# Nucleus search of attention rows: partial sums at two guessed points per row in place of three constants

## The reference

```python
def _adj_from_feats(Xa, W1, W2, W3):
    logits = (Xa @ W1) @ W2 @ (Xa @ W3).T
    idx = jnp.argsort(-logits, axis=1)
    csum = jnp.cumsum(jax.nn.softmax(jnp.take_along_axis(logits, idx, axis=1), axis=1), axis=1)
    k_i = jnp.sum(csum < 0.9, axis=1) + 1            # entries kept in this row
    keep = the k_i largest of each row
    return jax.nn.softmax(jnp.where(keep, logits, -jnp.inf), axis=1)
for s in range(2):
    A = _adj_from_feats(Xa, W1, W2, W3)
    Xf = Rf @ Xf;  Xb = Rb @ Xb;  Xa = A @ Xa
    Z = Z + (Xf @ U1[s] + Xb @ U2[s] + Xa @ U3[s])
```

## Time and profile before

| | |
|---|---|
| time, median of 3 runs | 3638.87 us (3638.29 to 3641.05) |
| span of the profiled execution | 3639.0 us |
| TensorE busy | 3175.4 us (87%) |
| VectorE busy | 2635.1 us (72%) |
| ScalarE busy | 1889.6 us (52%) |
| GpSimd busy | 996.2 us (27%) |
| L1345, evaluations, VectorE | 778.0 us, x208 |
| L1022, sums, ScalarE | 958.7 us, x312 |
| L1368 and L1378, extraction, VectorE | 586.9 us, x81 each |

### The profile page before, as it was taken

The page is one execution under the profiler, slowest core; times in us unless marked ns, Lnnn a source line. Parts: engine busy times, 40 slices in busy tenths (PEclk is TensorE's granted clock), DMA queues, the critical chain, the costliest instruction groups (busy, mean ns, idle before and its releaser), DMA issues. The chain is left out here.

```text
span 3639.0 us, 40362 instructions
## 1 busy us (share of the span) xinstructions
PE 3175.4 (87%) x13212; PEld 2289.6 (63%) x13212; DVE 2635.1 (72%) x3794; ACT 1889.6 (52%) x2355; POOL 996.2 (27%) x2293
## 2 busy tenths in 40 slices
PE   4999899987999999999875878667899889996799
PEld 3788688875677776777633445344555555554688
DVE  6963400006999999999839999999999999998100
ACT  2211311218788787888744556545565556563100
POOL 1212411211122221212211334334434334334211
PEclk9999999988999999999987989888999999998899
DMA  6544444432122221212221111111122222222255
GB/s 251 209 156 137 129 154 162 160 119 64 51 67 61 55 69 56 67 56 56 58 82 39 51 48 44 45 40 49 51 80 63 68 78 58 76 81 75 69 196 179
DMA packets 142416, 328.49 MB, mean 90 GB/s; under 512 B 15457, under 2 KB 95393, under 8 KB 130977
## 3 DMA queue, kind: packets, MB, share of 16 engines
q1 hardware_dynamic: 142240, 326.31, 28.3%
HBM read 287.59 MB, written 38.67 MB: 90 GB/s over the span
## 5 line engine op out<-in xcount | busy, mean ns | idle before, releaser
L1345 DVE SCALAR_TENSOR_TENSOR U<-E,trial 128x3327 f32<-128x3327 f32 x208 | 778.0, 3740 | 0.0
L880 PE MATMUL bank<-Hc,PT 128*128 128x256 f32 x2704 | 647.0, 392 | 68.8 <-ACT PT L1062 68.8
L880 PEld LDWEIGHTS bank<-Hc,PT 128*128 128x128 f32 x2704 | 528.0, 197 | 194.4 <-ACT PT L1062 92.3
L920 PE MATMUL bank<-big,adj 128*128 128x512 f32 x1352 | 613.7, 605 | 0.0
L1022 ACT ACTIVATE junk<-E,neg_3c 128x3327 uint8<-128x3327 f32 x156 | 479.1, 3071 | 5.1
L1022 ACT ACTIVATE junk<-E,neg_c 128x3327 uint8<-128x3327 f32 x156 | 479.6, 3074 | 1.7
L920 PEld LDWEIGHTS bank<-big,adj 128*128 128x128 f32 x1352 | 254.9, 194 | 329.4 <-issue 327.6
L893 PE MATMUL tr<-ident,E 128*128 128x128 f32 x1352 | 200.3, 291 | 275.5 <-DVE E L1394 275.5
L1062 ACT ACTIVATE PT<-tr 128x1024 f32<-128x1024 f32 x208 | 176.9, 851 | 369.2 <-PE tr L893 369.2
L893 PEld LDWEIGHTS tr<-ident,E 128*128 128x128 f32 x1352 | 172.8, 151 | 305.9 <-DVE E L1394 287.4
L920 PE MATMUL bank<-Hc,adj 128*128 128x256 f32 x1352 | 319.1, 388 | 0.0
(11 more groups left out here) (231 smaller groups left out, 4481.7 us busy)
## 6 DMA issues: line engine op xcount, KB each, us to landing
adj<-adjT SPq DMA_DIRECT2D x131, 448.0 KB, 3.4
E<-adjT SPq DMA_DIRECT2D x32, 1664.0 KB, 7.0
adj<-adjT SPq DMA_DIRECT2D x104, 384.0 KB, 3.4
adj<-adjT SPq DMA_DIRECT2D x20, 1664.0 KB, 7.0
adj<-adjT SPq DMA_DIRECT2D x14, 1216.0 KB, 5.7
E<-adjT SPq DMA_DIRECT2D x13, 1216.0 KB, 5.8
xt<-xin SPq DMA_DIRECT2D x52, 128.0 KB, 5.8
x_d<-xn SPq DMA_DIRECT2D x52, 128.0 KB, 1.7
```

The costliest lines, as they stand in the source:

```text
L880: last = mm(axp[:, 0:D], PT[k % 2][:, h, i * P:(i + 1) * P], Hc[:, j], start=(k == 0 and h == 0 and i == 0), stop=(k == SLOTS - 1 and h == ...
L920: last = mm(agg[:, 0:w], adj[:, j], rhs[:, j], start=(j == 0), stop=False)
L1345: V_.scalar_tensor_tensor(out=U[:, 0:N], in0=e, scalar=point, in1=e, op0=ALU.is_ge, op1=ALU.mult, accum_out=found))
```

## The change

ScalarE's six sums over E become four: Relu and Sign at two points, which are different for each row. GpSimd makes the first point (`guess`) from the mean of the scores, the maximum and the sum of exponentials, as soon as the exponential is done; after the first two sums it corrects it (`update(t, 0)`), ScalarE sums at the second point in slot 2, and `update(t, 1)` gives bracket and first point to VectorE. The mean comes from accumulators on the four copies of the scores. Slot 0 has no sums any more. VectorE evaluates 3 and 4 times, not 3 and 5, aims a little higher in step 1, and takes the mass above the upper end from an accumulator of L1355. GpSimd's order in a round changes: the 128x256 sums of z, y, x2 first, then `guess`, then the LayerNorm steps, `update(F, 0)`, the rest of the y LayerNorm, the z sums of step 0, `update(F, 1)`, and last the two 128x256 instructions of the output.

```diff
-EVALS = (3, 5)
-AIM = 3.0
-KEEP_END = 0.8
-FIXED = (0.008, 0.03, 0.1)
+EVALS = (3, 4)
+SUMS = 4
+POINTS = 2
+SHIFT = (1.4, 0.0)
+STEER = (2.0, 4.0)
+AIM = (3.0, 4.0)
+KEEP_END = (0.8, 0.75)
...
@@ ScalarE
-                        def fixed(t, lo, hi):
...
+                        def sums(t, j):
+                            act.wait_ge(aimed, POINTS * t + j + 1)
+                            for m, (func, acc_) in enumerate(((ACT.Relu, over), (ACT.Sign, sign))):
+                                before = SUMS * t + 2 * j + m
+                                if before >= 1:
+                                    act.wait_ge(summed, before)
+                                go(junk[:, 0:N], E[:, t % 3, 0:N], func, bias=negp[:, t % 2, j:j + 1], scale=1.0,
+                                   accum_out=acc_[:, t % 2, j:j + 1]).then_inc(summed, 1)
...
-                                    go(halves(E[:, L % 3])[:, :, c0:c0 + w], lg[:, :, 0:w], ACT.Copy).then_inc(lg_copied, 1)
+                                    go(halves(E[:, L % 3])[:, :, c0:c0 + w], lg[:, :, 0:w], ACT.Copy,
+                                       accum_out=musum[:, L % 2, k:k + 1]).then_inc(lg_copied, 1)
...
-                                    fixed(F, 0, 2)
...
-                                        fixed(F, 2, 4)
+                                        sums(F, 0)
...
-                                        fixed(F, 4, 2 * NF)
+                                        sums(F, 1)
...
@@ GpSimd
+                        def offer(t, j):
+                            then(ts(negp[:, t % 2, j:j + 1], p, -UNDER, None, ALU.mult))
+                            pool.sem_inc(aimed, 1)
...
+                        def prepare(step):
+                            then(ts(up_(0), p, STEER[step], ga_(12), ALU.mult, ALU.add),
+                                 ts(up_(1), p, AIM[step], ga_(12), ALU.mult, ALU.add),
+                                 ts(up_(2), p, RIDGE[step], None, ALU.mult))
+                            then(tt(up_(3), up_(2), up_(2), ALU.mult))
+                            then(tt(up_(4), up_(3), ga_(11), ALU.mult))
...
+                        def guess(t):
...
+                            pool.wait_ge(exp_done, t + 1)
...
+                            then(tt(ga[:, 0:2], musum[:, q, 0:2], musum[:, q, 2:4], ALU.add),
+                                 tt(ga_(2), z, root, ALU.pow))
+                            then(tt(ga_(3), ga_(0), ga_(1), ALU.add),
+                                 ts(ga_(4), ga_(2), ROOT, -ROOT - math.log(N), ALU.mult, ALU.add))
+                            then(ts(ga_(5), ga_(3), 1.0 / N, nm, ALU.mult, ALU.add))
+                            then(tt(ga_(6), ga_(4), ga_(5), ALU.subtract))
+                            then(ts(ga_(7), ga_(6), 2.0, 0.01, ALU.mult, ALU.add),
+                                 ts(ga_(8), ga_(5), 1.0, -SHIFT[step], ALU.mult, ALU.add))
+                            then(tt(ga_(9), ga_(7), half, ALU.pow),
+                                 tt(ga_(10), ga_(8), ga_(7), ALU.add))
+                            then(ts(ga_(13), ga_(9), -QUANTILE, ga_(10), ALU.mult, ALU.add))
+                            then(ts(ga_(14), ga_(13), -0.001, -36.0, ALU.min, ALU.max))
+                            then(tt(p, e_, ga_(14), ALU.pow))
+                            offer(t, 0)
...
+                        def update(t, j):
...
+                            pool.wait_ge(summed, SUMS * t + 2 * (j + 1))
+                            then(ts(count, sign[:, q, j:j + 1], 0.5, N / 2, ALU.mult, ALU.add))
+                            then(ts(mass_, count, p, over[:, q, j:j + 1], ALU.mult, ALU.add))
+                            then(tt(up_(15), mass_, up_(0), ALU.add),
+                                 tt(gap_p, mass_, up_(1), ALU.add),
+                                 ts(took[:, 1:2], mass_, tgt, None, ALU.is_ge))
+                            if j > 0:
...
+                                then(tt(ga_(11), up_(18), up_(19), ALU.mult))
...
+                            then(tt(up_(22), e_, up_(20), ALU.pow),
+                                 tt(ends, parts[:, 0], parts[:, 1], ALU.add))
+                            then(tt(up_(23), up_(22), p, ALU.mult))
+                            if j < POINTS - 1:
+                                then(ts(p, up_(23), hi, lo, ALU.min, ALU.max))
+                                offer(t, j + 1)
+                                prepare(step)
+                            else:
+                                then(ts(point, up_(23), hi, lo, ALU.min, ALU.max))
+                                pool.sem_inc(bracketed, 1)
...
+                            if F is not None:
+                                guess(F)
+                            if Y is not None:
+                                pool.wait_ge(ln3_a, 2 * Y + 1)
+                                tt(st3(1), st3(0), ln_const[:, 0:1], ALU.mult).then_inc(ln3_p, 1)
+                                ln_tail(st3, ln3_p, ln3_a, Y)
+                            if second(X):
+                                pool.wait_ge(ln_a, 2 * b + 1)
...
+                            if F is not None:
+                                update(F, 0)
+                            if second(X):
+                                ln_tail(st, ln_p, ln_a, b)
...
+                            if F is not None:
+                                update(F, 1)
...
@@ VectorE
-                            then(V_.tensor_copy(mass[:, 0:1], hi[:, 2:3]),
-                                 V_.memset(E[:, t % 3, N:NP], 0.0),
+                            then(V_.memset(E[:, t % 3, N:NP], 0.0),
                                  V_.scalar_tensor_tensor(out=U[:, 0:N], in0=e, scalar=hi[:, 0:1], in1=e,
-                                                         op0=ALU.is_ge, op1=ALU.subtract, reverse1=True))
+                                                         op0=ALU.is_lt, op1=ALU.mult, accum_out=sc[:, 5:6]))
+                            then(V_.tensor_tensor(mass[:, 0:1], Zs[:, q:q + 1], sc[:, 5:6], ALU.subtract))
```

More of the change, by code:

```diff
@@ L17 @@
+import math
 from contextlib import ExitStack, contextmanager
@@ L78, in pipeline @@
         static(u)
-def between_floats(value):
-    t = np.float32(3 * value)
-    while True:
-        t = np.nextafter(t, np.float32(np.inf))
-        near = [np.float32(t / np.float32(3))]
-        for _ in range(2):
-            near = [np.nextafter(near[0], np.float32(0))] + near + [np.nextafter(near[-1], np.float32(np.inf))]
-        if all(np.float32(3) * e != t and 3 * float(e) != float(t) for e in near):
-            return float(min(e for e in near if 3 * float(e) > float(t))), float(t)
 def build(nc, n_nodes, xin, adjT, W0T, b0, W1g, A1T, A2, A3, UA, UB, UC, gamma, beta, tin, Wg3, out):
@@ L1168, in _ @@
[L1168 to L1188 removed]
+                        ts = G_.tensor_scalar
@@ new lines, in _, with then @@
+                        pool.wait_ge(step_done, len(values))
+                        pool.sem_clear(step_done)
+                        root, minus, half, e_ = (known[:, i:i + 1] for i in range(4))
+                        ga_ = lambda a: ga[:, a:a + 1]
+                        up_ = lambda a: up[:, a:a + 1]
+                        p, gap_p = cand[:, 0:1], cand[:, 1:2]
+                        n = [0]
+                        def then(*ins):
+                            for i in ins:
+                                i.then_inc(step_done, 1)
+                            n[0] += len(ins)
+                            pool.wait_ge(step_done, n[0])
@@ L1189, in bracket @@
+                        def guess(t):
+                            q, step = t % 2, t // NT
+                            restart()
+                            z, nm = Zs[:, q:q + 1], nmax[:, q:q + 1]
+                            tgt, below = (trial2[:, q, a:a + 1] for a in (GOAL, BELOW))
+                            pool.wait_ge(exp_done, t + 1)
                             if t >= 2:
                                 pool.wait_ge(probs_ready, t - 1)
[L1192 to L1196 removed]
@@ L1197, in bracket @@
-                            then(tt(mid[:, :, 2], ft[:, 0], ft[:, 1], ALU.add))
-                            then(tt(mid[:, :, 1], mid[:, :, 2], tgt.to_broadcast([P, NF]), ALU.subtract),
-                                 tt(below, tgt, share[:, 4:5], ALU.mult),
-                                 G_.tensor_scalar(met[:, 1:NF + 1], mid[:, :, 2], tgt, None, ALU.is_ge))
-                            for i in range(2, NF + 1):
-                                then(tt(met[:, i:i + 1], met[:, i:i + 1], met[:, i - 1:i], ALU.mult))
@@ new lines, in guess @@
+                            then(tt(shape4(parts[:, 0]), zz, shape4(outset[:, 0]), ALU.mult),
+                                 ts(tgt, z, P_NUC, None, ALU.mult),
+                                 ts(ga_(12), z, -P_NUC, None, ALU.mult),
+                                 tt(ga_(15), z, minus, ALU.pow))
+                            then(tt(ends2[:, q], parts[:, 0], outset[:, 1], ALU.add),
```

(6 more changed lines are left out.)

200 lines of the change are left out of this document (81 added, 119 removed).

## The result

The changed kernel takes 3690.6 us (median; 3682.1 to 3691.2), the kernel before 3638.8 us beside it: a ratio of 1.0135 (95% interval 1.0120 to 1.0149), 52 us slower. The sign and the chain through GpSimd held; the loss was forecast five times too large. The profiled execution has a span of 3689.4 us, 50.5 more than the kernel before.

What follows compares the result with a forecast made beforehand. It took step 0 to be held by TensorE and VectorE, step 1 by VectorE. Adding +208 us for step 0, +41 for step 1 and 10 for first rounds to 3639 gave 3898, say 3900 us, range 3710 to 4030.

Steps and rivals of the forecast that it cites:

- The sign: Whole kernel: the change makes it slower, chance 0.86.
- the chain through GpSimd: Both steps: ScalarE's sums wait for GpSimd's guess and update, holding up TensorE and VectorE; +208 us and +41 us.
- The port rule: VectorE and GpSimd: a GpSimd instruction starting under a 3327-wide scalar_tensor_tensor ends with it; free under MAX8, MATCH_REPLACE, row maximum.
- The lengths of step 1's rounds: Step 1, search to search: 57.3 us with one extraction, 56.1 with two, 61.4 with three.
- Rival 2: GpSimd's steps cost only their own durations; chain 32.5 us, below TensorE's 36.54; 3519 us, chance 0.12.
- Rival 3: Points worse than the constants with one evaluation more: three extractions in every tile; 4160 us, half of that 4030; chance 0.06.
- Rival 1: The chain shows in step 0 only, step 1's longer search covers it; 3735 us, chance 0.10.
- the price of guess in step 0: GpSimd in step 0: guess up to its offer is 10 dependent steps, three with pow, 5.3 us.
- VectorE's windows: Step 0: guess advances only in 1.6 us gaps between evaluations, offer at 19.0 us; +208 us, 48 without windows so well filled.
- the case of cheaper steps: GpSimd's tensor_scalar at 0.19 us: some 2 us less per round over 50 rounds, -100 us.
- +41 forecast: Step 1: 1451 us against 1410 over 25 intervals; the saved evaluation is eaten by the chain.
- a second extraction would be nearly free: Step 1: a second extraction is covered by the chain; 56.1 us a round with two, 57.3 with one.

Runs made afterwards that it cites:

- act_tail_ln: Changed kernel with the first LayerNorm step ahead of guess and guess's last two steps (exponential, product) made by ScalarE; 3581.3 us, ratio 0.9831.
- cap_one: Changed kernel with exactly one extraction per tile and evaluations as tensor_scalar reading E once, counting entries, so not searching the right value; 3352.2 us.
- pad2: Changed kernel with two more dependent 128x1 multiplications in guess ahead of its last pow, 0.54 us of GpSimd work per tile; 3834.8 us, ratio 1.0540.
- cap_nowait: Changed kernel with exactly one extraction per tile and ScalarE's sums at constants 0.03 and 0.1, waiting for nothing of GpSimd, whose instructions all stay; 3544.5 us.
- best: act_tail_ln with GpSimd's three 128x256 instructions of y1 moved from ahead of guess to behind update(F, 0); 3576.6 us, ratio 0.9826.
- new_35: Changed kernel with EVALS = (3, 5), the evaluation given back in step 1; 3804.7 us, ratio 1.0450.
- ln_first: Changed kernel with one 128x1 GpSimd instruction, the first LayerNorm step of tile Y, moved ahead of guess; 3637.9 us, ratio 0.9994 to the kernel before.

## Why the prediction was wrong, and what of it held

**What held.** The port rule, read from three rows, holds in every run. In the kernel after, 229 of 230 GpSimd steps of at most six columns that started under a 3327-wide scalar_tensor_tensor, with over 0.7 us of it left, ended with it or later (the exception started 0.02 us after it; in no run did one get through that started more than 0.03 us after), and under MAX8, MATCH_REPLACE and the row maximum none took more than 0.57 us. The chain from the exponential over guess, sums, update, sums, update to the search holds, with its parts at the places named: ScalarE waits for the offer, the row maximum waits for the score copy, TensorE for PT. The lengths of step 1's rounds from search to search came out within 0.8 us, for one, two and three extractions. Rival 2 (faster, 3519 us) fell; act_tail_ln (3581 us) came nearest to it among the versions that do the whole search. Rival 3 fell: fewer extractions, not more. Rival 1 came nearest in time (3735 us), by amounts that were not the measured ones: it had +208 in step 0 and -112 in step 1, the runs +59 and -17.

**The step that failed: the price of guess in step 0, and with it the place of the offer in VectorE's windows.** I put 5.3 us on guess and 0.39 on each dependent tensor_scalar. Free of the port, guess takes 4.85 us, with tensor_scalars of 0.19 to 0.27 us and 0.08 behind each (cap_one). Half a microsecond is small, but the walk made of it an offer at 19.0 us into the search, caught under L1355, and hence an update caught under L1394. Measured, the offer was issued at 14.9, 0.02 us before the port closed, and the update ended 1.2 us before L1414 began (1702.68). The first update took 4.3 us (1697.18 to 1701.51) where 4.8 were put; by these rows even 4.8 would have ended 0.7 us before L1414, so this price was wrong too but did not decide. The round was 39.4 and not 46.2: 6.8 x 25 = 170 us, against an error of 149 in step 0 (208 forecast, 59 measured; the long rounds behind the tiles with two extractions take some of it back). pad2, which gives the half microsecond back, has rounds of 45.6.

That the windows decide was foreseen; on which side of them 0.02 us fell could not be known from the rows of before. But I had named the case of cheaper steps, and sized it wrongly: "some 2 us less per round" was the sum of the durations, where the same passage had just worked with windows. Pushed through the same windows, cheaper steps take 170 us off and not 100: 3898 - 170 = 3728 us, an estimate with the rounds that were measured since.

**Step 1: +41 forecast, -17 measured.** This is the smaller part of the error, 58 us, in two terms of nearly equal size. The full chain was put on all 25 intervals, but the output's LayerNorms and the seven 128x256 operations begin only some rounds into the step: the first five intervals took 251 us where 282 were forecast. The other twenty took 57.1 us on average, against 58.5, with 45 extractions, not 51. That a second extraction would be nearly free was right (from search to search 55.3 us with two, 56.7 with one). 149 and 58 are nearly all of the difference between the forecast's sum of 3898 and the measured 3690.6.

**What the profile was said to show.** Right: the lengths of step 1's steady rounds, the long instructions of GpSimd, the idle VectorE ahead of the row maximum, the waits of TensorE. Wrong: the wait of ScalarE for the first point is 6.5 us in the steady round, not 8 or more; and step 0 is not at 46 us, but for three rounds. Not foreseen: in cap_nowait GpSimd alone closes a loop of the same length, so the change's cost has two causes, one behind the other, and taking the first away (ScalarE's wait) brings next to nothing in step 0.

**Open.** Why the moved y1 work in best gave no more than 5 us is shown for the rounds with two extractions only, where VectorE hardly waits any more. How much of the 281 us of cap_one comes by the clock, what one-input evaluations would do in the kernel before, and whether the points or the new aim made four evaluations enough, is open as well. That a version with less of guess behind the port in both steps would reach the 37 and 44 us rounds of cap_one was not tried.

## What to carry over

Before small dependent steps are given to GpSimd, lay them on the timeline of VectorE's two-input instructions, not beside their own durations: each time the chain meets one it waits for its end (3.5 us here), and 0.02 us can decide whether it does. A forecast of such a chain is a set of discrete values, and its range has to hold those that a shift of half a microsecond gives. When an engine is idle but its instructions lie over a chain that they hold up, they are not free: in new_35 one more cost 5.0 of its 5.3 us, and moving the last link of the chain to ScalarE gave 57 us.

## What the runs showed that was not expected

0.54 us of GpSimd work cost 6.2 us per round and 144 us in all (pad2). Moving one 128x1 instruction gave 53 us (ln_first), moving two to ScalarE another 57 (act_tail_ln). In 22 rounds of step 0 two GpSimd steps were let through by 0.01 to 0.03 us each. And an evaluation of 5.3 us cost 5.0 us per round in rounds in which its engine waited 12 us (new_35).
